# Gate columns of z stored by DMAs of their own, and expert 2's weights loaded behind the second half of z

## The chip, the cores and the metric

The kernel runs on one core of a Trainium2 chip. The metric is the device time of one execution in microseconds; the median of several executions is compared. Five engines run their own instruction streams: TensorE (PE), VectorE (DVE), ScalarE (ACT), GpSimd (POOL) and SyncE (SP). SP computes nothing here; it issues most DMAs. They wait for each other by semaphores.

## What is computed

Two layers over x of 16 sequences by 256 tokens by 512 channels (4,096 tokens). The first is an adaptive layer norm and a gated feed-forward network with ternary weights. The second, in which the change lies, is a causal convolution along the sequence (taps from `cond_2048`) and a mixture of 8 experts, of which each token uses two:

```python
z = conv(x)                                   # [16, 256, 512]
logits = einsum('bsd,de->bse', z, Wr)
w, sel = top_k(logits, 2)
w = softmax(w)                                # the two gates of a token
out = x + sum over the token's two experts e of gate_e * (z @ We[e] + be[e])
```

## The kernel before

The first layer runs as a software pipeline over 32 tiles of 128 tokens. Then the convolution runs in 32 groups (`conv(r)`, r = 0 to 31, on TensorE; `evict(r)` on ScalarE copies each from PSUM into `ZS`). Groups 0 to 15 make half 0 of the batch (`ZS[0]`), groups 16 to 31 half 1 (`ZS[1]`). Each half is 2,048 rows of z, 16 in each of 128 partitions. Beside its 512 channels a row has two more columns (channel index D and D + 1) for the token's gates, which VectorE writes in `gates(h)` once the router is through. Rows of 514 words (`ZW`) go to the scratch `z_scratch` in DRAM, in three DMAs per half: `store_z(queue, h, part)` with channels 0 to 255, 256 to 383, and 384 to the end of the row. `z_out[h]` counts 16 for each DMA that has landed, so 48 is a whole half.

Meanwhile VectorE and TensorE build tables: the (token, expert) pairs are sorted by expert into 71 slots of 128 rows. `IDG` holds the row numbers of z to gather, `IDS` those of out to add to. Slots 0 and 1 may hold tokens of half 0 alone; `FLAG` says for each whether half 1 is needed too, as a value of `z_out[1]` to wait for (1 if not).

The slot loop (`over_slots`) runs over m = 0 to 70. GpSimd gathers 128 rows of z into one of 7 buffers `ZR` (`gather`, up to 6 ahead) and adds results to the output in DRAM (`scatter`). TensorE transposes the rows (`turn_r`, line 1740), ScalarE rounds them to `ZH` (`z_high`), VectorE makes the rest `ZL` (`z_low`), TensorE does 12 matmuls (line 1758), VectorE adds the bias into `YS` and ScalarE multiplies by the gate. Matmuls use weights as a high and a low part: `high(e)` on ScalarE (line 1054) and `low(e)` on VectorE (line 1358) make them from the raw weights `WRAW[e]`, one expert with each of the first slots. TensorE starts slot m below 8 only when `low(m)` is done.

SP loads the weights: `load_expert(e)`, four DMAs of 256 KB, one expert 1 MB. For e of 4 and above it waits for `high(e - 4)` (`wh_done`). Its order in this stretch is written by hand: three stores of half 0, a wait for `z_out[0]`, the bias table `BEB`, experts 1 and 0, the first store of half 1, expert 2, the waits for slots 0 and 1, a wait for `z_out[1]` of 49 (48 and one that SP adds itself), then experts 3 to 7. Weights may not come earlier since they lie where earlier data still lies. The other two stores of half 1 are issued by ScalarE between its copies. Behind the loads SP lets GpSimd's scatters go one by one (`rows_of`, `rows_free`).

Of the kernel before, what the change touches and what calls it, by code (L numbers as in the profile page):

```python
# [18 lines left out]
I32 = mybir.dt.int32  # L19
# [13 lines left out]
def adaln_ffn_moe(nc, x, cond, taps, rms_w, WkT, WoT, gamma, beta, w1T, w2T, w3T, Wr, We, be, out):  # L33
# [42 lines left out]
    with ctx:  # L76
# [278 lines left out]
        def store_z(queue, h, part):  # L355

            first, end = (GI * NJ * SPLIT[part + i] for i in range(2))
            if part + 2 == len(SPLIT):
                end = ZW
            queue.dma_start(bass.AP(z_d.tensor, h * BH * S * ZW + first, [[OB * ZW, P], [ZW, OB], [1, end - first]]),  # L360
                            ZS[h][:, :, first:end].bitcast(I32)).then_inc(z_out[h], 16)

        def piece_of(g):
# [62 lines left out]
        def _(sp):  # L426
# [190 lines left out]
            for part in range(3):  # L617
                sp.wait_ge(z_done, SPLIT[part + 1])
                if part == 2:
                    sp.wait_ge(gates_in, 1)  # L620
                store_z(sp, 0, part)
            sp.wait_ge(z_out[0], 48)
            sp.dma_start(BEB[:].rearrange("p e d -> p (e d)"), bass.AP(be.tensor, 0, [[0, P], [1, E * D]])).then_inc(be_in, 16)
            load_expert(1)
            sp.wait_ge(conv_done, NG + 7)
            load_expert(0)
            sp.sem_inc(z_out[1], 1)
            sp.wait_ge(z_done, NG + SPLIT[1])
            store_z(sp, 1, 0)
            sp.wait_ge(conv_done, NG + 11)  # L630
            load_expert(2)
            sp.wait_ge(slots_done, 1)
            halves = [sp.value_load(FLAG[0:1, m:m + 1], min_val=1, max_val=49) for m in range(LATE)]
            for half in halves:
# [4 lines left out]
            sp.wait_ge(first_done, 1)  # L639
            sp.wait_ge(z_out[1], 49)  # L640
            for e in range(3, E):
                load_expert(e)
# [20 lines left out]
        def _(pool):  # L663
# [197 lines left out]
            def gather(m):  # L861

                if m >= UZ:
                    pool.wait_ge(gate_done, m - UZ + 1)
                if m < LATE:
                    pool.wait_ge(z_free, m + 1)
                if m == LATE:
                    pool.wait_ge(z_out[1], 49)
                pool.indirect_dma_start(ZR[m % UZ][:, 0:ZW].bitcast(I32), None, z_d, bass.IndirectOffsetOnAxis(IDG[:, m:m + 1].bitcast(U32), 0)) \  # L869
                    .then_inc(zr_in[m % UZ], 16)  # L870
# [19 lines left out]
        def _(act):  # L890
# [167 lines left out]
            for r in range(2 * NG):  # L1058
# [22 lines left out]
                if r == 28:  # L1081
                    high(0)
            act.wait_ge(gates_in, 2)
            act.wait_ge(z_done, 2 * NG)
# [12 lines left out]
            def slot(m, i, _):  # L1097
                if m + 1 < MT and m + 1 != LATE:
                    z_high(m + 1, (i + 1) % UN)
                if m == 0:  # L1100
                    high(2)
                act.wait_ge(bank_read, m + 1)
                act.wait_ge(gate_done, m + 1)
                nc.scalar.activation(YS[i][:], YS[i][:], ACT.Copy, scale=SG2[i][:]).then_inc(ys_done, 1)  # L1104
                if m + 1 == LATE:
                    z_high(m + 1, (i + 1) % UN)
                if m + 3 < E:
                    high(m + 3)
# [5 lines left out]
        def _(dve):  # L1114
# [234 lines left out]
            def v(i):  # L1349

                step[0] += 1
                i.then_inc(route_v, 1)
                dve.wait_ge(route_v, step[0])
# [97 lines left out]
            v(nc.vector.tensor_tensor(HTOP[:, 0:UN], HTOP[:, 0:UN], IOSF[0:1, 1:UN + 1], ALU.is_lt))  # L1451
            v(nc.vector.tensor_scalar(FLAG[:], HTOP[:, 0:UN], 48.0, 1.0, ALU.mult, ALU.add))
            v(nc.vector.tensor_reduce(TEF[:], GE[:], AX.X, ALU.add))
# [350 lines left out]
```

## Time and profile before

| | us |
|---|---|
| median of 3 runs (822.41 to 827.26) | 823.74 |
| the profiled execution | 826.98 |
| its span in the trace | 824.9 |
| TensorE busy | 725.0 |
| VectorE busy | 532.0 |
| GpSimd busy | 503.9 |
| ScalarE busy | 437.5 |

The span runs from the first to the last recorded instruction; the execution's own time is 2.1 us more. TensorE's mean granted clock was 0.952 of full speed. Times within the trace are counted from the span's start. The profiled execution lies 3.2 us above the median of the three runs.

### The profile page before, as it was taken

To read this page: it belongs to the slowest core of one execution; us is meant where nothing else is said; L and a number is where in the kernel's file an instruction comes from. 1 tells how busy PE (TensorE), PEld (TensorE's weight loads), DVE (VectorE), ACT (ScalarE), POOL (GpSimd) and SP (SyncE) were. 2 spreads that over 40 slices of the span, in tenths; PEclk is the share of its full clock that TensorE was granted. 3 is DMA by queue.
4 is the path that set the end of the run, shared out by engine and by line. 5 is a ranking of instruction groups with operands and counts; after the bars stand their busy time and mean duration, and the time that the engine had idled before them with its cause. 6 is when DMAs were issued, how large, how long until landed. Compare 5 with 4: busy or idle time off the path is not lost.

```text
span 824.9 us, 13278 instructions
## 1 busy us (share of the span) xinstructions
PE 725.0 (88%) x3769; PEld 477.0 (58%) x3808; DVE 532.0 (64%) x765; ACT 437.5 (53%) x721; POOL 503.9 (61%) x760
## 2 busy tenths in 40 slices
PE   1753689999999999999999969995679999999995
PEld 0111235555555555565555559994558888888883
DVE  2466989898889888848876533576454445454542
ACT  2054457777778777847777511573443333434331
POOL 1036788787777777748773420003568888888773
PEclk9985889999999999989999988998799999999998
DMA  9986135566776766646667557698978989888983
GB/s 357 387 312 182 33 64 100 122 131 150 146 166 138 142 147 150 136 102 137 135 123 133 105 100 163 130 301 208 277 159 156 161 162 160 164 157 164 159 156 41
DMA packets 233113, 132.25 MB, mean 160 GB/s; under 512 B 182402, under 2 KB 198786, under 8 KB 231890
## 3 DMA queue, kind: packets, MB, share of 16 engines
q1 hardware_dynamic: 212866, 93.75, 46.8%
q0 software_dynamic: 15904, 35.48, 23.3%
q10 hardware_dynamic: 4272, 2.18, 1.3%
q8 instruction: 32, 0.52, 0.3%
q14 instruction: 39, 0.32, 0.1%
HBM read 74.44 MB, written 37.78 MB: 136 GB/s over the span
## 4 chain that ended last, share of the span: by engine, by line
PE 74%; DMA 10%; SPq 7%; DVE 3%; issue 2%; POOL 2%; ACT 1%; POOLq 0%; DVEq 0%; ACTq 0%
PE PS L1758 21%; PE PS L1615 12%; PE PS L1592 12%; PE PS L1604 12%; PE PS L1669 7%; PE PS L1636 3%; PE PS L1740 3%; DMA WRAW<-in_We 3%; SPq L429 3%; DMA WRT<-in_Wr 2%; PE PS L1645 2%; DMA z_scratch<-ZS 2%; PE PS L1627 2%; DMA QyT<-Qy 2%; SPq L515 1%
## 5 line engine op out<-in xcount | busy, mean ns | idle before, releaser
L1758 PE MATMUL PS<-W,ZH 128*128 x568 | 184.7, 406 | 7.1 <-DVE ZL L1498 7.0
L1592 PE MATMUL PS<-W,QyT 128*128 128x512 bf16 x499 | 126.0, 393 | 28.2 <-DMA QyT<-Qy 17.8
L869 POOL DMA_INDIRECT ZR<-z_scratch,IDG x71 | 78.9, 1112 | 94.6 <-DVE IDG L1466 60.6
L878 POOL DMA_INDIRECT out_x<-YS,IDS x71 | 112.7, 1587 | 39.3 <-issue 19.5
L1104 ACT ACTIVATE YS<-YS,SG 128x512 f32<-128x512 f32 x71 | 51.4, 724 | 138.5 <-DVE YS L1517 130.9
L1604 PE MATMUL PS<-W,QyT 128*128 128x512 bf16 x500 | 122.4, 384 | 0.6
L1758 PEld LDWEIGHTS PS<-W,ZH 128*128 128x128 f32 x568 | 103.1, 191 | 26.8 <-issue 8.4
L1615 PE MATMUL PS<-W,QT 128*128 128x512 bf16 x498 | 113.8, 379 | 0.7
L1498 DVE TENSOR_TENSOR ZL<-PS,ZH 128x512 fp32r<-128x512 f32 x71 | 49.1, 692 | 100.0 <-ACT ZH L1093 100.0
L1758 PE MATMUL PS<-W,ZL 128*128 x284 | 112.5, 396 | 0.0
L939 ACT ACTIVATE SG<-PS,sm 128x1024 f32<-128x1024 f32 x64 | 71.4, 1115 | 60.2 <-PE PS L1592 60.2
L1592 PEld LDWEIGHTS PS<-W,QyT 128*128 128x128 bf16 x512 | 51.1, 101 | 84.7 <-DMA QyT<-Qy 17.4
L1240 DVE TENSOR_TENSOR H<-SG,PS 128x1024 f32<-128x1024 f32 x64 | 77.8, 1216 | 21.3 <-PE PS L1604 19.6
L1604 PEld LDWEIGHTS PS<-W,QyT 128*128 128x128 bf16 x512 | 50.8, 99 | 62.8 <-issue 4.3
L945 ACT CAST Qh<-Ih 128x1024 bf16<-128x1024 int16 x64 | 66.8, 1043 | 34.7 <-DVE Ih L1254 34.7
L1615 PEld LDWEIGHTS PS<-W,QT 128*128 128x128 bf16 x512 | 50.2, 98 | 53.4
L1246 DVE TENSOR_REDUCE sm<-H 128x1 f32<-128x1024 f32 x64 | 78.1, 1220 | 2.2
L1669 PE MATMUL PS<-BD,XW 128*128 128x128 f32 x512 | 63.0, 285 | 8.0 <-DMA BD<-taps_scratch 7.8
L953 ACT ACTIVATE SG<-H 128x1024 f32<-128x1024 f32 x64 | 67.9, 1060 | 0.7 <-DVE H L1240 0.7
L1517 DVE TENSOR_TENSOR YS<-PS,BEB 128x512 f32<-128x512 f32 x71 | 49.1, 691 | 27.6 <-PE PS L1758 19.5
L1669 PEld LDWEIGHTS PS<-BD,XW 128*128 128x128 f32 x512 | 61.6, 201 | 8.7 <-DMA BD<-taps_scratch 8.2
L1758 PEld LDWEIGHTS PS<-W,ZL 128*128 128x128 f32 x284 | 54.1, 190 | 12.3
(249 smaller groups left out, 1110.9 us busy)
## 6 DMA issues: line engine op xcount, KB each, us to landing
X<-in_x SPq DMA_DIRECT2D x32, 256.0 KB, 10.0
out_x<-X SPq DMA_DIRECT2D x32, 256.0 KB, 2.5
WRAW<-in_We SPq DMA_DIRECT2D x32, 256.0 KB
ST<-out_x SPq DMA_DIRECT2D x28, 256.0 KB, 3.8
XR<-in_x SPq DMA_DIRECT2D x20, 256.0 KB, 3.6
stage<-in_w1T SPq DMA_DIRECT2D x4, 1024.0 KB, 8.0
stage<-in_w2T SPq DMA_DIRECT2D x4, 1024.0 KB
stage<-in_w3T SPq DMA_DIRECT2D x4, 1024.0 KB, 11.7
```

The source lines that it names most:

```text
L869: pool.indirect_dma_start(ZR[m % UZ][:, 0:ZW].bitcast(I32), None, z_d, bass.IndirectOffsetOnAxis(IDG[:, m:m + 1].bitcast(U32), 0)) \
L878: pool.indirect_dma_start(x1_d, bass.IndirectOffsetOnAxis(IDS[:, m:m + 1].bitcast(U32), 0), YS[m % UN][:], None, bounds_check=TOK - 1, oob ...
L939: nc.scalar.activation(SG[c][:], GP.rearrange("p a c -> p (a c)"), ACT.Silu, scale=OG[n % 2]).then_inc(silu_done, 1)
L945: nc.scalar.copy(Qh[:, half], Ih[:, half]).then_inc(qh_done, 1)
L953: nc.scalar.activation(SG[c][:], H[n % 2][:, half], ACT.Square, scale=FF ** -0.5, accum_out=(HSB if c else HSA)[n % 2]).then_inc(hsq_done, 1)
L1240: nc.vector.tensor_tensor(H[n % 2][:, half], SG[c][:], UP[c].rearrange("p a c -> p (a c)"), ALU.mult) \
L1246: nc.vector.tensor_reduce(HMC[n % 2][:, c:c + 1], H[n % 2][:, half], AX.X, ALU.max, apply_absolute_value=True).then_inc(hmc_done, 1)
L1592: i = nc.tensor.matmul(GP[:, a, :], QyT[t][:, k, :], W12[:, k, o:o + CH], start=(k == 0), stop=(k == KD - 1))
L1604: i = nc.tensor.matmul(UP[c][:, a, :], QyT[t][:, k, :], W12[:, k, o:o + CH], start=(k == 0), stop=(k == KD - 1))
L1615: i = nc.tensor.matmul(DN, QT[t][:, k, :], W3[:, k, :], start=(k == 0), stop=(k == KF - 1))
L1669: x = nc.tensor.matmul(bank[r % 4][:, P * i:P * i + P], rows, BD[:, GI * g + i, :, 1 - part, :], start=(part == 0), stop=(part == 1))
L1758: x = nc.tensor.matmul(bank[i], zz[i % 2][:, k, :], W2[:, bass.ds(q, 1), part, k, :].rearrange("p o d -> p (o d)"), start=(k == 0 and n == ...
```

## The change

The last piece of a half of z now ends with channel 511, and the two gate columns of all 2,048 rows go in a DMA of their own, `store_gates`, with runs of 8 bytes. A half is whole at 64 instead of 48, with SP's own increment 65 for half 1. SP no longer waits for the gates before the third piece, nor does ScalarE. SP stores the gates of half 0 behind the three pieces, those of half 1 behind expert 0's load and ahead of the first piece. Expert 2 is loaded no more between the first piece and the wait for half 1, but first behind that wait. On ScalarE `high(2)` moves behind the gating of slot 0, and `high(3)` to slot 1.

```diff
@@ -355,10 +355,13 @@
         def store_z(queue, h, part):
 
             first, end = (GI * NJ * SPLIT[part + i] for i in range(2))
-            if part + 2 == len(SPLIT):
-                end = ZW
             queue.dma_start(bass.AP(z_d.tensor, h * BH * S * ZW + first, [[OB * ZW, P], [ZW, OB], [1, end - first]]),
                             ZS[h][:, :, first:end].bitcast(I32)).then_inc(z_out[h], 16)
+
+        def store_gates(queue, h):
+
+            queue.dma_start(bass.AP(z_d.tensor, h * BH * S * ZW + D, [[OB * ZW, P], [ZW, OB], [1, ZW - D]]),
+                            ZS[h][:, :, D:ZW].bitcast(I32)).then_inc(z_out[h], 16)
 
         def piece_of(g):
 
@@ -616,29 +619,29 @@
 
             for part in range(3):
                 sp.wait_ge(z_done, SPLIT[part + 1])
-                if part == 2:
-                    sp.wait_ge(gates_in, 1)
                 store_z(sp, 0, part)
-            sp.wait_ge(z_out[0], 48)
+            sp.wait_ge(gates_in, 1)
+            store_gates(sp, 0)
+            sp.wait_ge(z_out[0], 64)
             sp.dma_start(BEB[:].rearrange("p e d -> p (e d)"), bass.AP(be.tensor, 0, [[0, P], [1, E * D]])).then_inc(be_in, 16)
             load_expert(1)
             sp.wait_ge(conv_done, NG + 7)
             load_expert(0)
             sp.sem_inc(z_out[1], 1)
+            sp.wait_ge(gates_in, 2)
+            store_gates(sp, 1)
             sp.wait_ge(z_done, NG + SPLIT[1])
             store_z(sp, 1, 0)
-            sp.wait_ge(conv_done, NG + 11)
-            load_expert(2)
             sp.wait_ge(slots_done, 1)
-            halves = [sp.value_load(FLAG[0:1, m:m + 1], min_val=1, max_val=49) for m in range(LATE)]
+            halves = [sp.value_load(FLAG[0:1, m:m + 1], min_val=1, max_val=65) for m in range(LATE)]
             for half in halves:
                 sp.wait_ge(z_out[1], half)
                 sp.sem_inc(z_free, 1)
             sp.wait_ge(conv_done, 2 * NG)
             sp.wait_ge(tab_done, NK // CC)
             sp.wait_ge(first_done, 1)
-            sp.wait_ge(z_out[1], 49)
-            for e in range(3, E):
+            sp.wait_ge(z_out[1], 65)
+            for e in range(2, E):
                 load_expert(e)
 
             def rows_of(m, i, _):
@@ -865,7 +868,7 @@
                 if m < LATE:
                     pool.wait_ge(z_free, m + 1)
                 if m == LATE:
-                    pool.wait_ge(z_out[1], 49)
+                    pool.wait_ge(z_out[1], 65)
                 pool.indirect_dma_start(ZR[m % UZ][:, 0:ZW].bitcast(I32), None, z_d, bass.IndirectOffsetOnAxis(IDG[:, m:m + 1].bitcast(U32), 0)) \
                     .then_inc(zr_in[m % UZ], 16)
 
@@ -1080,7 +1083,6 @@
                     store_z(nc.scalar, 1, 1)
                 if r == 28:
                     high(0)
-            act.wait_ge(gates_in, 2)
             act.wait_ge(z_done, 2 * NG)
             store_z(nc.scalar, 1, 2)
             high(1)
@@ -1097,14 +1099,16 @@
             def slot(m, i, _):
                 if m + 1 < MT and m + 1 != LATE:
                     z_high(m + 1, (i + 1) % UN)
-                if m == 0:
-                    high(2)
                 act.wait_ge(bank_read, m + 1)
                 act.wait_ge(gate_done, m + 1)
                 nc.scalar.activation(YS[i][:], YS[i][:], ACT.Copy, scale=SG2[i][:]).then_inc(ys_done, 1)
                 if m + 1 == LATE:
                     z_high(m + 1, (i + 1) % UN)
-                if m + 3 < E:
+                if m == 0:
+                    high(2)
+                if m == 1:
+                    high(3)
+                if 1 <= m < E - 3:
                     high(m + 3)
 
             over_slots(slot)
@@ -1449,7 +1453,7 @@
             v(nc.vector.tensor_reduce(HTOP[:, 0:UN], HSUM[:], AX.X, ALU.add))
             v(nc.vector.tensor_scalar(HTOP[:, 0:UN], HTOP[:, 0:UN], HEND[:, 0:1], 1.0 / P, ALU.add, ALU.mult))
             v(nc.vector.tensor_tensor(HTOP[:, 0:UN], HTOP[:, 0:UN], IOSF[0:1, 1:UN + 1], ALU.is_lt))
-            v(nc.vector.tensor_scalar(FLAG[:], HTOP[:, 0:UN], 48.0, 1.0, ALU.mult, ALU.add))
+            v(nc.vector.tensor_scalar(FLAG[:], HTOP[:, 0:UN], 64.0, 1.0, ALU.mult, ALU.add))
             v(nc.vector.tensor_reduce(TEF[:], GE[:], AX.X, ALU.add))
             v(nc.vector.tensor_scalar(TEF[:], TEF[:], float(E - 1), None, ALU.min))
             v(nc.vector.tensor_copy(TEXP[:], TEF[:]))
```

SP's queue around the stores of z. `ZS_70` and `ZS_71` are the halves 0 and 1, `WRAW_121`, `WRAW_122`, `WRAW_123` and `WRAW_124` the raw weights of experts 0, 1, 2 and 3. Before:

```order
L360 DMA z_scratch<-ZS_70 2048x1x256 [waits z_done]
L360 DMA z_scratch<-ZS_70 2048x1x128 [waits z_done]
L360 DMA z_scratch<-ZS_70 2048x1x130 [waits gates_in,z_done]
L623 DMA BEB<-in_be 128x4096 [waits z_out0]
L614 DMA WRAW_122<-in_We 128x1x512 x4
L614 DMA WRAW_121<-in_We 128x1x512 [waits conv_done]
L614 DMA WRAW_121<-in_We 128x1x512 x3
L360 DMA z_scratch<-ZS_71 2048x1x256 [waits z_done]
L614 DMA WRAW_123<-in_We 128x1x512 [waits conv_done]
L614 DMA WRAW_123<-in_We 128x1x512 x3
```

With the change:

```order
L358 DMA z_scratch<-ZS_70 2048x1x256 [waits z_done]
L358 DMA z_scratch<-ZS_70 2048x1x128 [waits z_done] x2
L363 DMA z_scratch<-ZS_70 2048x1x2 [waits gates_in]
L626 DMA BEB<-in_be 128x4096 [waits z_out0]
L617 DMA WRAW_122<-in_We 128x1x512 x4
L617 DMA WRAW_121<-in_We 128x1x512 [waits conv_done]
L617 DMA WRAW_121<-in_We 128x1x512 x3
L363 DMA z_scratch<-ZS_71 2048x1x2 [waits gates_in]
L358 DMA z_scratch<-ZS_71 2048x1x256 [waits z_done]
```

A gate store with runs of 2 words (2048x1x2) now stands behind the third piece of half 0 and another ahead of the first piece of half 1, and expert 2's four DMAs have left this place. They stand behind the wait for half 1, where before the first expert was the third:

```order
L614 DMA WRAW_124<-in_We 128x1x512 [waits z_out1,first_done,tab_done,conv_done]
L614 DMA WRAW_124<-in_We 128x1x512 x3
L614 DMA WRAW_125<-in_We 128x1x512 [waits wh_done]
```

and now it is the second:

```order
L617 DMA WRAW_123<-in_We 128x1x512 [waits z_out1,first_done,tab_done,conv_done]
L617 DMA WRAW_123<-in_We 128x1x512 x3
L617 DMA WRAW_124<-in_We 128x1x512 x4
L617 DMA WRAW_125<-in_We 128x1x512 [waits wh_done]
```

ScalarE's instructions from the last store of z to the third slot; `W_120` are the split weights, `YS_129` and `YS_130` the results of slots 0 and 1, `ZH_133` and `ZH_134` the two buffers of `z_high`. Before:

```order
L360 DMA z_scratch<-ZS_71 2048x1x130 [waits z_done,gates_in]
L1054 CAST W_120<-WRAW_122 128x2048 [waits w_in1_1]
L1093 CAST ZH_133<-PS 128x512 [waits trz_done]
L1093 CAST ZH_134<-PS 128x512 [waits trz_done]
L1054 CAST W_120<-WRAW_123 128x2048 [waits w_in1_2]
L1104 ACTIVATE YS_129<-YS_129,SG_207 128x512 [waits gate_done,bank_read]
L1054 CAST W_120<-WRAW_124 128x2048 [waits w_in1_3]
L1104 ACTIVATE YS_130<-YS_130,SG_208 128x512 [waits gate_done,bank_read]
L1093 CAST ZH_133<-PS 128x512 [waits exp_done,trz_done]
L1054 CAST W_120<-WRAW_125 128x2048 [waits w_in1_0]
```

With the change:

```order
L358 DMA z_scratch<-ZS_71 2048x1x128 [waits z_done]
L1057 CAST W_120<-WRAW_122 128x2048 [waits w_in1_1]
L1095 CAST ZH_133<-PS 128x512 [waits trz_done]
L1095 CAST ZH_134<-PS 128x512 [waits trz_done]
L1104 ACTIVATE YS_129<-YS_129,SG_207 128x512 [waits gate_done,bank_read]
L1057 CAST W_120<-WRAW_123 128x2048 [waits w_in1_2]
L1104 ACTIVATE YS_130<-YS_130,SG_208 128x512 [waits gate_done,bank_read]
L1095 CAST ZH_133<-PS 128x512 [waits exp_done,trz_done]
L1057 CAST W_120<-WRAW_124 128x2048 [waits w_in1_3]
L1057 CAST W_120<-WRAW_125 128x2048 [waits w_in1_0]
```

The cast of expert 2 (`WRAW_123`) has moved behind the gating of slot 0, that of expert 3 (`WRAW_124`) behind slot 1's gating and slot 2's `ZH`.

## Rows read from the trace of the kernel before

**Rows 1.** The page: the chain that ended last.

```profile
PE 74%; DMA 10%; SPq 7%; DVE 3%; issue 2%; POOL 2%; ACT 1%; POOLq 0%; DVEq 0%; ACTq 0%
```

**Rows 2.** The chain in order of time, 552 to 616 us: start, us, what.

```profile
558.81 12.90 DMA z_scratch<-ZS
...
573.68 6.47 DMA WRAW<-in_We
...
580.74 1.91 ACT W L1054
...
585.14 19.07 DMA WRAW<-in_We
...
611.06 3.01 PE PS L1758 x12
614.07 0.44 PE PS L1740 x4
```

**Rows 3.** Windows: busy time by engine, TensorE clock, DMA share, GB/s.

```profile
527.00:532.20 5.20, 5.20 (x49) 5.20 (x49) 1.77 (x4) 1.76 (x3) 0.00 (x0) 1.00 1.05 204
532.20:535.00 2.80, 2.80 (x28) 2.80 (x27) 2.77 (x4) 1.43 (x5) 0.00 (x0) 1.00 0.01 2
540.00:548.00 8.00, 8.00 (x87) 8.00 (x86) 6.11 (x12) 5.67 (x29) 0.00 (x0) 1.00 1.05 260
556.00:560.00 4.00, 2.10 (x19) 1.91 (x18) 3.79 (x9) 1.80 (x3) 2.73 (x2) 1.00 1.09 371
569.20:573.00 3.80, 3.80 (x24) 2.90 (x23) 2.35 (x4) 0.73 (x1) 1.03 (x1) 1.00 0.07 10
573.00:580.00 7.00, 1.15 (x6) 0.61 (x4) 1.79 (x2) 0.00 (x0) 5.71 (x5) 0.93 0.94 240
597.00:604.50 7.50, 5.51 (x28) 4.17 (x26) 5.13 (x5) 3.38 (x5) 4.88 (x3) 1.00 1.08 278
```

**Rows 4.** Timeline of SP's queue of DMA issues, 507 to 586 us.

```profile
507.66 18.70 SPq L360 DMA_DIRECT2D z_scratch<-ZS  x3
...
533.88 7.13 SPq L614 DMA_DIRECT2D WRAW<-in_We  x8
541.25 0.55 SPq L360 DMA_DIRECT2D z_scratch<-ZS  x1
547.04 5.10 SPq L614 DMA_DIRECT2D WRAW<-in_We  x4
...
571.80 14.08 SPq L614 DMA_DIRECT2D WRAW<-in_We  x20
```

**Rows 5.** DMA view, packets in 70:72, 510:515, 527:529 and 530:532 us, in that order.

```profile
DMA packets 1946, 0.33 MB, mean 166 GB/s; under 512 B 1841, under 2 KB 1841, under 8 KB 1946
...
DMA packets 1532, 1.57 MB, mean 314 GB/s; under 512 B 0, under 2 KB 1532, under 8 KB 1532
...
DMA packets 1107, 0.58 MB, mean 288 GB/s; under 512 B 0, under 2 KB 1107, under 8 KB 1107
...
DMA packets 539, 0.28 MB, mean 138 GB/s; under 512 B 9, under 2 KB 539, under 8 KB 539
```

**Rows 6.** Timelines: gates on VectorE, slots on TensorE, first scatter on GpSimd.

```profile
521.30 0.18 DVE L1406 TENSOR_TENSOR ZS<-P,P 128x16 f32<-128x16 f32 x1
...
527.79 0.18 DVE L1406 TENSOR_TENSOR ZS<-P,P 128x16 f32<-128x16 f32 x1
...
584.60 1.22 PE L1758 MATMUL PS<-W,ZH 128*128 x2
...
591.07 0.72 PE L1758 MATMUL PS<-W,ZH 128*128 x2 [0.88 <-DVE ZL L1498]
...
595.61 0.72 PE L1758 MATMUL PS<-W,ZH 128*128 x2 [1.10 <-DVE ZL L1498]
...
607.48 0.72 PE L1758 MATMUL PS<-W,ZH 128*128 x2 [3.06 <-DVE ZL L1498]
...
586.91 1.63 POOL L878 DMA_INDIRECT out_x<-YS,IDS  x1 [6.98 <-SPq L654]
```

## The prediction

> **What bounds the kernel now.** I began with the page: TensorE holds 74% of the chain that ended last [rows 1]. So a change that touches no matmul can matter only where that chain leaves TensorE. The chain in order of time shows where [rows 2]: between the end of the convolution (558.1) and the expert loop at full pace (611.1) it runs through the last store of z (12.90 us), expert loads (6.47 us) and, longest of all, the last expert load (19.07 us). Behind it stand a cast on ScalarE, the cast ZH of the slot and a subtraction on VectorE, and then the loop, whose 12 matmuls and 4 transposes make 2.75 + 0.44 us a slot with nothing between them.
>
> So the end of the kernel is: the moment at which expert 7's weights land (604.2), plus a fixed tail. `high(7)` stands ahead of the ZH cast of slot 6, so slot 6 starts 3.3 us after the landing (607.48 [rows 6]). Slots 6 to 70 follow at about 3.2 us whatever came before. Whatever delays the landing delays the end by as much.
>
> What sets the landing? The windows of the DMA engines [rows 3]: they are full from before 540 on (1.05 in 540 to 548, 1.09 in 556 to 560) until 569.2, then comes a hole of 3.8 us (0.07, the store's completion and the first loads' issue), then 573 to 604.5 at 0.94 to 1.08. Between two holes (532.2 to 535 and 569.2 to 573) the path is, as I read it, one line of bytes. The SP queue shows what they are [rows 4]: behind BEB experts 1 and 0 (eight DMAs), the 2 MB piece of z half 1, expert 2, then from 571.80 experts 3 to 7. Let T be the time when z half 1 is complete (571.71, end of the 12.90 us in [rows 2]); the five loads end 32.5 us behind it.
>
> **The change part by part.** There are two gate stores, each of 2,048 rows of 8 B, where before these 8 B rode at the end of 520 B rows. And expert 2's load moves from in front of T to behind it.
>
> *Gate store of half 0.* The gates were written by 521.5 and the issue of the third z store of that half ended at 526.4 [rows 4], so before the store did not wait for them [rows 6]; nothing is gained by taking that wait away. The new store is issued behind the last piece on the same queue, and BEB and experts 1 and 0 wait for all four stores. Its price g0 lies fully on the path. No row shows 8 B writes. From below: near 70 to 72 us a window of the DMA view holds 1,841 packets under 512 B [rows 5], nearly all of the 2,048 writes of 64 B to g_scratch, in about 1.5 us; I take 1.4 us as the lower bound. From above: in the tail of the last z store 539 packets pass in 2 us [rows 5], 270 a microsecond; the 1 KB pieces of 510 to 515 pass at 306 a microsecond (1,532 in 5 us), so the pace there goes by the packet more than by the byte. 2,048 at about 300 a microsecond make 6.8 us. The gate store follows such a tail directly, but an 8 B row touches one place in memory where a 512 B row off its boundary has two ragged ends. I take 3.1 us, the middle of the two in ratio.
>
> *Gate store of half 1.* The gates are there at 528.0 [rows 6], long before SP comes to it (541), so no wait. It stands before the 2 MB piece in a stretch that is full [rows 3]. It follows loads, not stores, so the first thousand or so packets may pass quickly, as the first 1,107 of the last z store did in 2 us [rows 5]. I take g1 = 2.0 us, bounds 0 and 6.8. The rows of 512 instead of 520 B save 1.5% of two 5.2 us stores at most, 0.2 us, left out.
>
> *Expert 2 out of the stretch before T.* It is 512 packets of 2 KB. Where it ran (556 to 560) the engines moved 371 GB/s, against 204 GB/s in the z store alone and 260 GB/s in loads alone [rows 3]: loads and stores overlap well there. At the rate of loads alone it is worth 1.05 MB / 260 = 4.0 us. But the two 1 MB pieces of z behind it, alone, take 5.2 us each (527.0 to 532.2), together 10.4 us, against 13.2 us from 556.0 to 569.2 with it and with two gathers. So no more than 2.8 us can be saved, and if the gathers are not hidden about 0.7. I take 1.7 us. The last piece is issued at 558.8 and still finds the previous one in transit.
>
> *Expert 2 behind T.* Now it goes alone with other loads, in a stretch at share 0.94 to 1.08: 4.0 us at 260 GB/s, 2.5 if one gather and scatter less fall in the stretch, 4.3 at the 240 GB/s of 573 to 580 [rows 3]. I take 4.0.
>
> *The new order on ScalarE and the waits.* `high(2)` now waits for a load that is issued after T, and behind it stand YS of slot 1, ZH of slot 2 and `high(3)`; VectorE's `low(2)` holds YS of slot 1 as well. Expert 2 should land as expert 3 did, T + 9.0 [rows 2]; cast 1.9, subtraction 2.3, YS twice 1.4, ZH 0.6, ZL 0.7: slot 2's matmuls begin at T + 16, before at T + 12.9 (584.60). With slots 4.5 us apart (591.07 to 595.61 [rows 6]) slot 6 could begin at T + 34; expert 7 allows it at T + 32.5 + 4.0 + 3.3 = T + 39.8. So this costs nothing while the loads keep more than 5 us of lead. Load 7 waits for `high(3)`, T + 18; at that time at least two loads are still queued. The scatters wait behind load 7 on SP (the first started at 586.91 after 6.98 us of waiting [rows 6]); they start some 5 us later and GpSimd's loop of 3.2 us a slot has no slack, but the last six slots have no gathers, which gives it back.
>
> **The sum.** 3.1 + 2.0 − 1.7 + 4.0 = +7.4 us. The profiled execution took 826.98 us (span 824.9), so 834.4; it lies 3.2 us above the median of 823.74, so the prediction for the median is 831.1 us.
>
> The Trainium skill (DMA: Bandwidth & Descriptors, Specifications) says that below 512 B a DMA engine reads, modifies and writes, and that only from 512 B on is line rate reached; this speaks against gate stores. The 64 B writes of [rows 5] don't agree at full strength; no run here shows it for 8 B.
>
> **The rivals.**
> - *Every 8 B row costs a full packet of a throttled store* (6.8 us each): 6.8 + 6.8 − 1.7 + 4.0 = +15.9 us, 839.6. For it: the pace of the tail barely depends on size. Against: the fast 64 B writes. Chance 0.15. This is what the page's rule would do here.
> - *Cheap gate stores*: 1.4 + 0 to 1.4, and expert 2 takes 2.8 out and puts 2.5 to 4.0 in: +1.1 to +4.0, about 826.3; no change that can be measured (under 0.5%, 4.1 us). Chance 0.25.
> - *Faster*: the stretch behind T is held by the landing of single loads and by gathers, not by bytes, so that expert 2 slips into it. Its issue is 2.5 us on a queue that was done at 585.9, 18 us ahead of the last landing. Then T comes sooner by all of expert 2's 4.0 us, the gate rows hide in the completion of the stores, the shorter rows give their 0.2, and the end comes 4.2 us sooner: 819.5. It decides only if expert 2 costs well under 1 us behind T and the gates nothing. Against it: share 1.08 in 597 to 604.5. Chance 0.07.
> - *The slot chain takes over*: if loads come quicker than thought, slot 6 waits at T + 34 for the chain, not for expert 7. This gives no more than 5 us back and is inside the spread of the first case.
> - My forecast, +4.1 to +12: chance 0.53.
>
> **How the numbers follow.** Slower by over 0.5% is 0.53 + 0.15 = 0.68, same 0.25, faster 0.07. The range: down to 824.5 in the cheap case, up to 838.0, which leaves out the faster case and most of the dear one. The first case alone spans 828 to 836.
>
> **What would show it.** Half 0's z_out complete 3 us later, BEB issued near 536.6; more than 2,048 extra packets under 512 B there. T at 571.7 + 3.1 + 2.0 − 1.7 = 575.1. Expert 7 landing near 611.6, 36.5 us behind T, slot 6 at 615. The loop at 3.19 us a slot. I am wrong if T falls before 570, if expert 7 lands less than 34 us behind T, or if a gate store takes under 1.4 or over 6.8 us.

## The result and the profile after

The changed kernel takes 830.55 us (median of 7 executions, 828.53 to 833.06). The kernel before, with four more executions beside the three that I knew, takes 826.13 (median of 7; 825.7 without one disturbed execution of 987 us, which the ratio leaves out). The ratio is 1.0065 with an interval of [1.0047, 1.0083], which is +5.4 us [+3.9, +6.9]. The change makes the kernel slower, by 2 us less than I said.

The profiled execution takes 830.38 us, its span is 828.4 us: +3.5 us in the span against the profile of before. This is less than the +5.4 us of the medians because the profiled execution of before was itself a slow one (826.98 us, against 823.74 and, in later sets of 18 to 23 executions, 824.65, 825.42 and 826.58). So a difference between the two traces understates the change by about 2 us, and the timings decide the sizes. Each kernel has one trace; what follows from a trace alone is a single execution.

The page: the chain by engine, and the counts of DMA packets.

```profile
PE 75%; DMA 9%; SPq 7%; DVE 4%; issue 2%; POOL 2%; ACT 1%; POOLq 0%; DVEq 0%; ACTq 0%
DMA packets 237241, 132.25 MB, mean 160 GB/s; under 512 B 186530, under 2 KB 202914, under 8 KB 236018
```

The chain has the make-up of [rows 1]. Packets are up by 4,128 (from 233,113), two lots of 2,048 and a few, while the bytes are the same.

SP's queue, the answer to [rows 4]:

```profile
506.65 19.73 SPq L358 DMA_DIRECT2D z_scratch<-ZS  x3
526.42 1.65 SPq L363 DMA_DIRECT2D z_scratch<-ZS  x1
535.80 0.35 SPq L626 DMA_DIRECT2D BEB<-in_be  x1
536.19 5.94 SPq L617 DMA_DIRECT2D WRAW<-in_We  x8
542.26 0.55 SPq L363 DMA_DIRECT2D z_scratch<-ZS  x1
542.85 9.47 SPq L358 DMA_DIRECT2D z_scratch<-ZS  x1
573.00 20.22 SPq L617 DMA_DIRECT2D WRAW<-in_We  x24
```

The third piece is issued at the same moment as before (526.38 against 526.36). BEB, which needs all of half 0 landed, starts at 535.80 instead of 533.49: 2.3 us later. That is gate store 0. Half 1 is whole at 573.0 instead of 571.8: 1.2 us later, so half of the delay has been given back before T. Six loads instead of five follow.

One line shows something that I had not reckoned with. Behind the gate store of half 1 the issue of the first piece of z takes 9.47 us, where before it took 0.55 [rows 4]. It ends at 552.3 instead of 541.8, and the DMA engines have a hole: their share is 0.35 from 551 to 552, where before it is 1.18. The run with this gate store alone shows the same (an issue of 6.32 us, shares of 0.44 and 0.42 from 548 to 550). Why SP is held there no run shows.

Windows one microsecond wide over the end of half 0's stores, with the columns of [rows 3] (before first, then after):

```profile
531.00:532.00 1.00, 1.00 (x11) 1.00 (x11) 1.00 (x1) 0.17 (x1) 0.00 (x0) 1.00 0.90 93
532.00:533.00 1.00, 1.00 (x12) 1.00 (x11) 0.96 (x3) 0.59 (x1) 0.00 (x0) 1.00 0.12 17
```

```profile
531.00:532.00 1.00, 1.00 (x12) 1.00 (x11) 1.00 (x1) 0.20 (x1) 0.00 (x0) 1.00 1.49 85
532.00:533.00 1.00, 1.00 (x12) 1.00 (x11) 0.96 (x3) 0.59 (x1) 0.00 (x0) 1.00 1.13 24
533.00:534.00 1.00, 1.00 (x12) 1.00 (x11) 1.00 (x2) 0.00 (x0) 0.00 (x0) 1.00 0.09 1
534.00:535.00 1.00, 1.00 (x12) 1.00 (x11) 0.96 (x2) 0.81 (x4) 0.00 (x0) 1.00 0.00 0
```

This is what 8 B rows look like: the engines are busy (1.13 to 1.49) while 24 to 85 GB/s pass (the first of the two windows still holds some 512 B rows). In before 0.12 was left for 532 to 533, so the data ended near 532.1; here it ends just behind 533, about 1 us later. Then next to nothing moves until SP sees the half complete at 535.80, 2.7 us, against 1.3 to 1.4 us before (532.1 to 533.49). So gate store 0 costs about one microsecond of rows and another between the last row and the semaphore. The Trainium skill (DMA: Bandwidth & Descriptors, Anatomy of one DMA, told there for GpSimd's path) says that most of a DMA's fixed 2 us is the write's receipt, since the semaphore waits until the last byte has landed. The trace agrees in kind, with 1.3 us before and 2.7 us behind 8 B rows. Why the wait is longer behind 8 B rows is not shown. I had priced the rows alone.

The chain from the end of the convolution, the answer to [rows 2]:

```profile
558.78 14.13 DMA z_scratch<-ZS
...
580.04 13.42 DMA WRAW<-in_We
...
595.28 0.59 ACT ZH L1095
595.89 0.70 DVE ZL L1502
596.73 4.60 PE PS L1762 x12
...
602.81 1.90 ACT W L1057
604.71 0.49 ACT ZH L1095
605.22 0.70 DVE ZL L1502
606.06 3.01 PE PS L1762 x12
...
614.55 3.00 PE PS L1762 x12
```

The last store takes 14.13 instead of 12.90 us. The long load of 19.07 us is gone from the chain: now it goes from a load through the slots, matmuls at half clock among them (4.60 us). That looks like the rival of the slot chain. But ScalarE's timeline shows a near tie:

```profile
602.81 1.90 ACT L1057 CAST W<-WRAW 128x2048 fp32r<-128x2048 f32 x1
604.62 0.57 ACT L1095 CAST ZH<-PS 128x512 fp32r<-128x512 f32 x1
606.73 0.72 ACT L1104 ACTIVATE YS<-YS,SG 128x512 f32<-128x512 f32 x1 [1.54 <-DVE YS L1521]
607.73 1.91 ACT L1057 CAST W<-WRAW 128x2048 fp32r<-128x2048 f32 x1 [0.27 <-DMA WRAW<-in_We]
```

`high(7)` begins at 607.73 and still waited 0.27 us for expert 7's load; the slot chain had let it go at 607.45. Before, it began at 604.23 after 1.86 us of waiting for the load. In the changed kernel the load still comes last, by 0.27 us. From this cast to the end of the span both kernels take the same: 828.4 − 607.73 = 220.67 us and 824.9 − 604.23 = 220.67 us. So the +3.5 us are all ahead of this cast.

### The profile page after: what moved, and what is told of

The parts are those of the page before. It is cut to its first block, busy times and chain, and to the rows that moved or that the text cites. A ratio compares the mean times of both kernels' runs of the same rounds, so it can differ in the third digit from the quotient of the medians.

```text
span 828.4 us, 13278 instructions
## 1 busy us (share of the span) xinstructions
PE 726.2 (88%) x3769; PEld 478.4 (58%) x3808; DVE 533.2 (64%) x765; ACT 437.5 (53%) x721; POOL 501.1 (60%) x760
## 4 chain that ended last, share of the span: by engine, by line
PE 75%; DMA 9%; SPq 7%; DVE 4%; issue 2%; POOL 2%; ACT 1%; POOLq 0%; DVEq 0%; ACTq 0%
PE PS L1762 22%; PE PS L1619 12%; PE PS L1596 12%; PE PS L1608 12%; PE PS L1673 7%; PE PS L1744 3%; PE PS L1640 3%; SPq L432 3%; DMA WRT<-in_Wr 2%; DMA z_scratch<-ZS 2%; PE PS L1649 2%; DMA WRAW<-in_We 2%; PE PS L1631 2%; DMA QyT<-Qy 1%; SPq L518 1%
## 5 line engine op out<-in xcount | busy, mean ns | idle before, releaser
L1596 PE MATMUL PS<-W,QyT 128*128 128x512 bf16 x499 | 124.8, 391 | 27.7 <-DMA QyT<-Qy 15.9
L881 POOL DMA_INDIRECT out_x<-YS,IDS x71 | 117.6, 1656 | 43.9 <-SPq L657 23.2
L872 POOL DMA_INDIRECT ZR<-z_scratch,IDG x71 | 71.9, 1013 | 96.3 <-DVE IDS L1479 62.7
L1596 PEld LDWEIGHTS PS<-W,QyT 128*128 128x128 bf16 x512 | 50.8, 100 | 83.4 <-DMA QyT<-Qy 15.6
```

The costliest lines, as they stand in the source:

```text
L881: pool.indirect_dma_start(x1_d, bass.IndirectOffsetOnAxis(IDS[:, m:m + 1].bitcast(U32), 0), YS[m % UN][:], None, bounds_check=TOK - 1, oob ...
L1596: i = nc.tensor.matmul(GP[:, a, :], QyT[t][:, k, :], W12[:, k, o:o + CH], start=(k == 0), stop=(k == KD - 1))
```

## The experiments

Effects are (ratio − 1) times the median of before in the same set of executions, with the interval. The differences shown are cut; `...` marks what is left out.

**The gate stores alone.** Expert 2 and ScalarE's casts where they were; both gate stores as in the change.

Against the changed kernel:

```diff
             store_gates(sp, 1)
             sp.wait_ge(z_done, NG + SPLIT[1])
             store_z(sp, 1, 0)
+            sp.wait_ge(conv_done, NG + 11)
+            load_expert(2)
...
-            for e in range(2, E):
+            for e in range(3, E):
                 load_expert(e)
...
```

> The kernel before with the two gate stores of the change, expert 2 loaded and cast where it was. Theory A (the DMA engines are full from BEB to the last expert load, so all that is added there is paid): half 0 costs the 2.3 us by which BEB's issue moved in the changed kernel (533.49 to 535.80), half 1 about 1.3 us of its 8-byte rows; +3.6 us against before, that is the whole loss of the changed kernel (+3.5 in the span). Theory B (the gate store of half 1 is hidden and the moved load costs the rest): +2.3 us. Theory C (most of the loss is the move): under +1.5 us.

Measured: 829.63 us, ratio 1.0055 [1.0040, 1.0070], +4.5 us [+3.3, +5.8]. Most of the loss is here, and theory C is out. The trace is of the slowest execution of its set (833.5 us), and T comes 17.65 us behind the issue of the last store, against 12.90. In these 17.65 us SP's queue moved 2.74 MB, against 0.13 MB before: the late first piece of z and expert 2 stood there together.

**The move alone.** The kernel before, with expert 2 behind T and the change's order on ScalarE.

```diff
-            sp.wait_ge(conv_done, NG + 11)
-            load_expert(2)
...
-            for e in range(3, E):
+            for e in range(2, E):
                 load_expert(e)
...
```

> The kernel before with expert 2 loaded behind the wait for half 1 and the changed order on ScalarE, no gate stores. Theory A: T comes some 2.4 us sooner (569.3 instead of 571.7) and the last expert lands 2.3 us later counted from T, so -0.1 us against before, no change. Theory B: +1.2 us. Theory C: +2 to +3.5 us. My prediction's own terms gave +2.3 us.

Measured: 825.89 us, ratio 1.0012 [0.9993, 1.0032], +1.0 us [−0.6, +2.6]. This can't tell theory A (−0.1), B (+1.2) and my own terms (+2.3) apart. The sum with the run above is 5.5 us, and the change itself measured 5.4: the parts add, within some 2 us. The chain shows what the move gains:

```profile
559.85 9.04 DMA z_scratch<-ZS
```

Without expert 2 in front the last store takes 9.04 instead of 12.90 us: 3.9 us gained, where I had bounded the gain by 2.8. ScalarE's queue (q10), which carries the second and the last piece, shows why: packets, MB and share from the issue of the last store to its end, first before, then the move alone:

```profile
q10 hardware_dynamic: 3676, 1.88, 77.2%
```

```profile
q10 hardware_dynamic: 2234, 1.15, 64.2%
```

The last piece has 2,048 rows. So some 1,600 rows of the second piece were still to come before, and some 170 here. The 1,442 fewer packets at the 365 a microsecond of 529 to 531 us before (729 packets in 2 us) are an estimate of 4.0 us.

Behind T expert 2 costs less than I thought. The last cast stands 34.2 us behind T (603.39 − 569.15, the start of the gather that waits for half 1), before 32.3 (604.23 − 571.97): +2.0 us. The queues from T to the landing of expert 7, SP's loads (q1) and GpSimd's gathers and scatters (q0), again before and then the move alone:

```profile
q1 hardware_dynamic: 2880, 5.24, 60.8%
q0 software_dynamic: 1212, 3.17, 38.9%
```

```profile
q1 hardware_dynamic: 3456, 6.29, 71.0%
q0 software_dynamic: 993, 2.66, 30.4%
```

The loads are 1.05 MB more, but gathers and scatters 0.51 MB less, since the first scatter starts 20.0 us behind T instead of 14.9 (589.14 and 586.91). At the mean of 260 GB/s that both stretches have, the other 0.54 MB are 2.1 us, the measured 2.0.

So in this trace the stretch from the last store to the last cast is 1.9 us shorter (43.5 against 45.4), yet the span is 0.3 us longer. The last store was issued 1.0 us later, as was half 0's third piece (527.39 against 526.36), which the edit does not touch, and the tail behind the last cast is 1.1 us longer by TensorE's clock, as told below. The timings do not show the 1.9 us as a gain; whether the slower tail belongs to the move is open.

**The gate store of half 0 alone**, against the kernel before.

```diff
-            if part + 2 == len(SPLIT):
+            if part + 2 == len(SPLIT) and h == 1:
                 end = ZW
...
-                if part == 2:
-                    sp.wait_ge(gates_in, 1)
                 store_z(sp, 0, part)
-            sp.wait_ge(z_out[0], 48)
+            sp.wait_ge(gates_in, 1)
+            sp.dma_start(bass.AP(z_d.tensor, D, [[OB * ZW, P], [ZW, OB], [1, ZW - D]]),
+                         ZS[0][:, :, D:ZW].bitcast(I32)).then_inc(z_out[0], 16)
+            sp.wait_ge(z_out[0], 64)
```

> The kernel before with a gate store for half 0 alone. Theory A and B: +2.3 us, BEB issued near 535.8. Theory C: under +1 us. With the first run of this call the difference is the price of half 1's gate store: 1.3 us by A, 0 by B.

Measured: 829.21 us, ratio 1.0048 [1.0026, 1.0071], +4.0 us [+2.1, +5.9]. SP's queue:

```profile
504.51 20.83 SPq L360 DMA_DIRECT2D z_scratch<-ZS  x3
525.38 1.66 SPq L621 DMA_DIRECT2D z_scratch<-ZS  x1
534.54 0.35 SPq L624 DMA_DIRECT2D BEB<-in_be  x1
```

From the end of the third piece's issue (525.34) to BEB it is 9.2 us; before 7.1 (526.36 to 533.49), in the changed kernel 9.4. So in the trace this store costs 2.1 to 2.3 us, at the lower end of the timed interval. In this trace 1,991 packets under 512 B pass from 530 to 532, about 1,000 a microsecond, against the 365 a microsecond of 520 B rows in the tail before: an 8 B row costs much less of the engines than such a row. What makes the timed +4.0 larger than the trace's price stays open.

**The changed kernel with the old order of casts on ScalarE.**

```diff
+                if m == 0:
+                    high(2)
                 act.wait_ge(bank_read, m + 1)
...
-                if m == 0:
-                    high(2)
-                if m == 1:
-                    high(3)
-                if 1 <= m < E - 3:
+                if m + 3 < E:
                     high(m + 3)
```

> The changed kernel with ScalarE's order of before (high(2) ahead of YS of slot 0, high(3) behind it, high(4) behind slot 2's ZH). Theory A (the landing of expert 7 rules): within 1 us of the changed kernel, +3.5 us against before. Rival D (the slot chain rules, since in the changed kernel YS of slot 4 ended at 607.4 and the cast of expert 7 began at 607.7; two casts in a row hold up slot 3's ZH): 2 to 4 us faster than the changed kernel, or slower if ZH of slot 2 now waits for expert 3.

Measured: 830.46 us, ratio 1.0068 [1.0045, 1.0090], +5.6 us [+3.7, +7.4]: the changed kernel within the noise (830.55). At the end the order on ScalarE makes no difference beyond some 2 us. In between it does: slot 2's matmuls begin at 592.37 instead of 588.51, 18.8 us behind T instead of 15.6. The last cast (608.11) then waits for no load any more: here the slot chain has taken over.

**Half 0's gates ahead of its third piece**, against the changed kernel. Between the second and the third piece the DMA engines have time, so I expected the gate rows to be nearly free there.

```diff
+                if part == 2:
+                    sp.wait_ge(gates_in, 1)
+                    store_gates(sp, 0)
                 sp.wait_ge(z_done, SPLIT[part + 1])
                 store_z(sp, 0, part)
-            sp.wait_ge(gates_in, 1)
-            store_gates(sp, 0)
```

> The changed kernel with half 0's gate store issued ahead of the third piece, where the DMA engines stand idle (525.5 to 527) and the gates are ready (521.5). Theory A' (half 0's gate store costs what it costs, about 4 us by the run of half 0 alone, because it stands last before BEB; the rest of the change costs 1 to 1.5 us): BEB issued 2 us earlier than in the changed kernel, and +1 to +1.5 us against before instead of +5.4. Rival (8-byte rows slow whatever store stands near them): +3 us or more.

Measured: 829.92 us, ratio 1.0055 [1.0033, 1.0076], +4.5 us [+2.7, +6.3]. The expectation of +1 to +1.5 us failed, and the rival (+3 us or more) has it. The queue and three windows:

```profile
522.02 0.51 SPq L363 DMA_DIRECT2D z_scratch<-ZS  x1
526.36 0.51 SPq L358 DMA_DIRECT2D z_scratch<-ZS  x1
535.03 0.35 SPq L627 DMA_DIRECT2D BEB<-in_be  x1
```

```profile
525.00:526.00 1.00, 1.00 (x12) 1.00 (x11) 0.93 (x3) 0.26 (x1) 0.00 (x0) 1.00 1.44 66
526.00:527.00 1.00, 1.00 (x12) 1.00 (x11) 0.90 (x5) 0.33 (x1) 0.00 (x0) 1.00 0.39 3
...
528.00:529.00 1.00, 1.00 (x11) 1.00 (x10) 0.27 (x2) 0.12 (x1) 0.00 (x0) 1.00 1.22 198
```

The gate rows are done by 526.5, before the third piece starts. Yet the third piece now moves 198 GB/s from 528 to 529, where in before and after it moved 293 and 299 GB/s: its quick start is lost. From its issue (526.87) to BEB it takes 8.2 us, against 7.1 before. So only about half of the trace's price is recovered, and the times (+4.5 against +5.4, each with some 2 us of uncertainty) can't tell whether anything was. The last cast (605.06) waited for no load here either.

**Half 0's gate store twice**, the second into a spare place of the same shape, against the kernel before. Beside the edit of half 0's gate store alone:

```diff
+            sp.dma_start(bass.AP(spare_d.tensor, D, [[OB * ZW, P], [ZW, OB], [1, ZW - D]]),
+                         ZS[0][:, :, D:ZW].bitcast(I32)).then_inc(z_out[0], 16)
...
```

> The kernel before with half 0's gate store, and the same store once more to a spare place in DRAM, both waited for. If the price of a gate store is that of its 2,048 packets (10 to 17 ns each on 16 engines, 1.3 to 2.2 us), BEB is issued another 1.3 to 2.2 us later than with one gate store and the time rises by as much over it: +5.5 to +6 us against before. If the price is the longer completion behind a throttled store, the second adds under 0.7 us. If each 8-byte row costs what a 512-byte row costs in the tail, the second adds 6.8 us.

Measured: 832.46 us, ratio 1.0084 [1.0062, 1.0105], +6.9 us [+5.1, +8.7]; 2.9 us more than one store, with about 2.6 us of uncertainty on that difference.

```profile
525.52 1.65 SPq L622 DMA_DIRECT2D z_scratch<-ZS  x1
527.22 4.41 SPq L624 DMA_DIRECT2D spare_scratch<-ZS  x1
537.51 0.35 SPq L627 DMA_DIRECT2D BEB<-in_be  x1
```

From the third piece to BEB it is 12.0 us (525.48 to 537.51), 2.8 more than with one. Here time and trace agree on some 2.8 us for a second store of 2,048 rows of 8 B behind the first. That is above the 1.3 to 2.2 us of the first theory in the trace; the other two (under 0.7 us, and 6.8 us) are out.

**The gate store of half 1 alone.** The same edit as for half 0, in the place that the change gives it.

```diff
-            if part + 2 == len(SPLIT):
+            if part + 2 == len(SPLIT) and h == 0:
                 end = ZW
...
+            sp.wait_ge(gates_in, 2)
+            store_gates(sp, 1)
             sp.wait_ge(z_done, NG + SPLIT[1])
             store_z(sp, 1, 0)
...
```

> The kernel before with a gate store for half 1 alone. The difference of the two earlier runs (gate stores of both halves +4.5 us, of half 0 alone +4.0) makes half 1's store worth +0.5 us: ratio 0.9995 to 1.002, T (the second gather's start) 0 to 1 us after that of before when both are counted from the last z store's issue (13.2 to 14.2 us). Rival: the 3.3 us by which that stretch was longer in the one profile with both stores (17.9 against 14.6) is the price, and something else in that run gave it back: +3 us, ratio 1.0035 to 1.0045, 16 us from the store to the second gather. The forecast had 2.0 us.

Measured: 827.80 us, ratio 1.0013 [0.9999, 1.0026], +1.1 us [−0.1, +2.1]. From the last store to the second gather it is 14.0 us (559.45 to 573.46), before 13.2. So this store costs about 1 us, and the 3 us of the rival are out as the price of this store alone. The 17.9 us in the trace of both gate stores are 2.5 us more than the two single traces add up to (0.8 and 1.4 us over 13.2); the times show no such excess.

**Half 0 with rows of 64 B instead of 8 B.** As the run with half 0's gate store alone, but it takes the last 14 channels too.

```diff
-            if part + 2 == len(SPLIT) and h == 1:
-                end = ZW
+            if part + 2 == len(SPLIT):
+                end = ZW if h == 1 else D - 14
...
-            sp.dma_start(bass.AP(z_d.tensor, D, [[OB * ZW, P], [ZW, OB], [1, ZW - D]]),
-                         ZS[0][:, :, D:ZW].bitcast(I32)).then_inc(z_out[0], 16)
+            sp.dma_start(bass.AP(z_d.tensor, D - 14, [[OB * ZW, P], [ZW, OB], [1, ZW - D + 14]]),
+                         ZS[0][:, :, D - 14:ZW].bitcast(I32)).then_inc(z_out[0], 16)
```

> As the run with half 0's gate store alone, but the gate store takes the last 14 channels too: 2,048 rows of 64 B in place of 8 B, and 456 B in place of 512 B in the third piece. Theory, a row costs what it costs whatever its length up to 64 B: the same +4.0 us (ratio 1.0035 to 1.006), BEB issued 9.2 us behind the third piece's issue. Rival 1, it is the write of a few bytes that is dear and 64 B are cheap, as the 64 B writes to g_scratch were: BEB 7.5 to 8.0 us behind, +1 us. Rival 2, the price goes with bytes: BEB 9.5 to 10, +4.5 us or more.

Measured: 829.72 us, ratio 1.0042 [1.0025, 1.0059], +3.5 us [+2.1, +4.9].

```profile
525.77 1.57 SPq L621 DMA_DIRECT2D z_scratch<-ZS  x1
535.62 0.35 SPq L624 DMA_DIRECT2D BEB<-in_be  x1
```

BEB comes 9.9 us behind the third piece, 0.7 more than with 8 B rows; the times can't tell the two apart. The 9.9 us lie where the second rival (the price goes with bytes) had put them, the +3.5 us where the theory had. But a price by bytes would be eight times as high, and this one is 2.8 us in place of 2.1, so most of it is that of 2,048 rows, and filling them would not help. The first rival, that writing few bytes is the dear part, does not hold: it gave 7.5 to 8.0 and +1 us. One thing else changed: the third piece now has rows of 456 B in place of 512 B, and what that alone costs was not measured.

**The other direction: 2,048 rows fewer.** If rows are what counts, the kernel before should gain by storing half 1 in two pieces of 256 channels instead of three, with the counts waited for changed to match.

```diff
+            split = SPLIT if h == 0 else [0, 8, 16]
...
-                if r == NG + SPLIT[2] - 1:
-                    act.wait_ge(z_done, r + 1)
-                    store_z(nc.scalar, 1, 1)
```

> The kernel before with half 1 of z stored in two pieces of 8 groups (4,096 rows of 1,024 and 1,032 bytes) instead of three (6,144 rows of 1,024, 512 and 520), the second issued behind the last copy at 558.8. Theory A (stores go by the packet): 2,048 packets fewer, T 2 to 3 us sooner (569 to 570), expert 7 as much sooner: -2 us against before. Rival (stores go by the byte, or the last piece of twice the size starts too late): T at 571.7 or later, no gain or up to 2 us lost.

Measured: 823.89 us, ratio 0.9989 [0.9974, 1.0003], −0.9 us [−2.1, +0.2].

```profile
558.29 9.70 DMA z_scratch<-ZS
...
602.73 4.40 PE PS L1756 x12
```

The last store takes 9.70 instead of 12.90 us although it is twice as large, so T is 3.2 us sooner (counted from the store). ScalarE's queue from its issue to its end:

```profile
q10 hardware_dynamic: 2064, 2.11, 69.3%
```

Only its own rows pass there. That is 2.11 MB in 9.70 us, where before 1.88 MB in 3,676 packets took 12.90. The last cast starts at 599.48 instead of 604.23. But the next slot runs at half clock, 4.40 us instead of 3.0, and the span is 3.6 us shorter (821.3). Of this 2.2 us are the choice of executions: the profiled one of before lies 1.6 us above the median of before in this set (825.42), this one 0.6 below its own. What is left is 1.5 us between the medians, and the ratio gives 0.9. The theory's −2 us lie at the edge of the interval: the trace shows T sooner, the times do not show a gain.

**Two pieces and the move together** (the edits of both).

> The kernel of two pieces with expert 2 loaded behind T and the changed order on ScalarE. Theory A: with both out of the way the engines run dry before the last piece is issued at 558.8, so T cannot fall under 558.8 + 1.5 + 6.6 + 2 = 569, and expert 2's 2 to 4 us behind T are paid in full: +1 to +3 us over the two pieces alone. Rival (the move is free as it was on the kernel before): the same as the two pieces alone.

Measured: 824.57 us, ratio 0.9994 [0.9980, 1.0007], −0.5 us [−1.7, +0.6].

```profile
554.00:562.00 8.00, 5.77 (x51) 5.37 (x49) 7.31 (x24) 4.42 (x5) 3.79 (x2) 1.00 0.29 65
...
559.85 9.65 DMA z_scratch<-ZS
```

With expert 2 gone the DMA engines stand at 0.29 from 554 to 562, so there is room in front of the last store, and it still takes 9.65 us. The move then only adds work behind T: the last cast is 33.8 us behind it instead of 31.2. The median is 0.7 us above that of the two pieces alone; the +1 to +3 us of theory A and the rival's nothing can't be told apart. No version measured is faster than the kernel before with an interval that excludes no change.

## Why the prediction was right, and where its sizes were off

| step | said, us | measured, us |
|---|---|---|
| gate store of half 0 | +3.1 | +4.0 [+2.1, +5.9] timed; BEB +2.1 to +2.3 |
| gate store of half 1 | +2.0 | +1.1 [−0.1, +2.1] timed |
| expert 2 out from before T | −1.7 | −3.9 in one trace |
| expert 2 behind T | +4.0 | +2.0 in that trace, +2.3 in after |
| both moves together | +2.3 | +1.0 [−0.6, +2.6] timed |
| sum | +7.4 | +5.4 [+3.9, +6.9] timed; +3.5 between the traces |

*The number itself: partly luck.* I said 831.1 us and measured 830.55. But I had added to a median of 823.74 from three executions, and the kernel before takes 825.7 without the disturbed one; this 2 us and the 2 us by which the effect was too large cancel. The effect is the test: +7.4 said, +5.4 measured.

*What bounds the kernel: right, but only just.* Landing of expert 7 and a fixed tail: the tail behind the last cast is 220.67 us in both kernels. In the changed kernel the load came last by 0.27 us only, and in the runs with the old casts and with the early gate store the last cast waited for no load.

*The waits taken away: right.* The third piece is issued at 526.38 against 526.36; nothing was gained by not waiting for the gates.

*Gate store 0: right within its bounds, by a different make-up.* I priced rows passing the engines. The trace shows about one microsecond of these, and another between the last row and the semaphore. The rival in which each row costs as much as a full packet of a throttled store (6.8 us each, 15.9 in all) is out: a second such store adds 2.8 us, both gate stores together cost 4.5, and 8 B rows pass at about 1,000 a microsecond, not 300.

*Gate store 1: 2.0 was too much.* It stands among loads in a stretch with other work, and about 1.1 us of it reach the end. Its interval just takes in my value. I priced rows again; the late issue of the first piece and the hole behind it were not in my terms.

*Expert 2 out of the stretch before T: the step that was mis-sized.* I took 1.7 us and held that no more than 2.8 could be saved, since the two pieces of z alone would take 5.2 us each from 556.0 on. But without expert 2 the second piece does not start there: it had moved 993 packets by 557 in the run of the move alone, against 3 by 556 before (both 2.8 us ahead of the last store). So at the issue of the last store its rows were nearly through, and that store took 9.0 instead of 12.9 us: 3.9 us.

*Expert 2 behind T: mis-sized too.* 1.05 MB at 260 GB/s are 4.0 us, but the stretch grew by 2.0 to 2.3. The scatters, which wait behind the last load on SP, start later (the first at 594.24 instead of 586.91 in the changed kernel), so less of GpSimd's traffic falls in the stretch: 2.51 MB instead of 3.17. The stretch carries 8.82 MB instead of 8.44, at 254 instead of 260 GB/s. I had this case at 2.5 us and took the other. The two errors, −2.2 and −1.7 to −2.0 us, go the same way: by the traces the move should gain 1.9 us (−3.9 + 2.0). Timed it costs +1.0 [−0.6, +2.6], 1.3 less than I said. Why the times do not show this gain stays open.

*ScalarE's order: right.* Slot 2's matmuls begin 15.6 us behind T (588.51), where I said 16, and putting the old order back, which delays slot 2 by 3.9 us, changes nothing that can be measured at the end.

*The rivals.* Cheap gate stores (+1.1 to +4.0): the lower end of the interval, 3.9 us, touches it, but the middle is above. Faster: out, T did not come sooner and expert 2 did not vanish. The slot chain takes over: it ties.

*What would show it.* BEB I put at 536.6 (535.80), T at 575.1 (573.0), expert 7 landing 36.5 us behind T (34.7), slot 6 at 615 (610.98). T stayed above 570 and the landing over 34 us behind it. But the third sign did come: a gate store under 1.4 us, that of half 1 with +1.1 [−0.1, +2.1]. T came 2.1 us sooner than said and the landing another 1.8 us sooner behind it, and the profiled execution took 830.38 us where I had said 834.4: by the traces I was 4.0 us too high, by the times 2.0.

## What to carry to other kernels

The last 8 bytes of a wide row, put in a DMA of their own, cost by the row. Here 2,048 such rows cost 2 to 4 us where someone waits for them and about 1 us among other transfers, and rows of 64 B could not be told from them in time. Before pricing a transfer by its bytes, count the rows that still stand in its queue, and ask what else leaves the stretch when it enters: these were my two large errors.

## What the runs showed of the hardware

**Rows counted more than bytes for the last store.** From its issue to its end 1.88 MB in 3,676 packets took 12.90 us (before) and 2.11 MB in 2,064 packets 9.70 us (two pieces). In full flow rows of 520 B passed at 365 a microsecond (190 GB/s, 529 to 531 in before) and rows of 1,032 B at 321 (343 GB/s, 562 to 568 in two pieces and the move): twice the bytes in a row for an eighth fewer rows. That store took 9.65 us there, and 9.04 in the move alone with 2,048 rows of 520 B; the second still had some 170 rows of the piece before it in front, so the two are not a clean pair.

**A store right behind the gate rows had no quick start.** With the gate rows just done, the next store moved 198 GB/s from 528 to 529, without them 293. Whether the small rows do this, or the shorter pause (about 1 us without transfers instead of 1.7), no run tells apart.

**TensorE's clock makes the tail of some traces about 1.2 us longer.** In the profiles of before, after, the changed kernel with the old casts, the early gate store, the double gate store and the 64 B rows, slot 6 ran at full clock (3.0 us for its 12 matmuls). In those of the gate stores alone, the move alone, half 0's and half 1's gate store alone, two pieces, and two pieces with the move, it ran at 1.2 GHz for most of its length (4.3 to 4.6 us). With half 0's gate store alone, the chain shows it so:

```profile
608.99 4.59 PE PS L1759 x12
```

The granted clock there is 0.60 (608.5 to 612), where the same slot of before has 1.00. In the six slow cases TensorE had waited 2.0 to 4.6 us ahead of the slot; after, the old casts, the early gate store and the 64 B rows, which kept the clock, had waited 1.1 to 1.5 us. But before waited 3.06 us [rows 6] and the double gate store 2.65, and both kept it, so the length of this wait alone does not decide. The tail behind the last cast is 221.8 to 222.0 us with the slow slot; without it, it is 220.7 to 220.8, and 221.2 in the run with the early gate store. Each kernel has one trace, so no run tells whether the fall goes with the kernel or with the execution. A difference of one microsecond between two profiles of this kernel can be just that.
